# Moving the first score products and the last transposes of u ahead in the full turns of a pipelined language-model tower

## What is computed

```python
h = take(quantised_table, x)
n = layernorm(h)
# mixer on rms(n):
proj = rms(n) @ in_proj_w.T                  # z gate, u, B, C, dt
u, B, C = silu(causal_conv4(u, B, C))        # B and C normalised
z_t = (z + d*(B u - A*y)) / (1 + d*d*A); y_t = y + d*z_t; out = sum(y*C)   # scan over 128 tokens
n = n + (out + D*u) * silu(zgate) @ out_proj_w.T + out_proj_b
n = n + gelu(rms(n) @ fc1_w.T + fc1_b) @ fc2_w.T + fc2_b
h = h + n
out = h + int8_linear(layernorm(h))          # one scale from the largest |value| of all
```

## Time and profile before

| | |
|---|---|
| three executions, us | 1285.45, 1287.50, 1288.92 |
| median | 1287.5 |
| profiled execution | 1287.84 |
| its span, first to last instruction | 1286.0 |
| PE busy | 1149.3 (89%) |
| DVE busy | 1112.5 (87%) |
| ACT busy | 789.0 (61%) |
| POOL busy | 715.1 (56%) |
| mean granted PE clock | 0.990 |

### The profile page before, as it was taken

The page is one execution under the profiler, slowest core; times in us unless marked ns, Lnnn a source line. Parts: engine busy times, 40 slices in busy tenths (PEclk is TensorE's granted clock), DMA queues, the critical chain, the costliest instruction groups (busy, mean ns, idle before and its releaser), DMA issues. The chain is left out here.

```text
span 1286.0 us, 25011 instructions
## 1 busy us (share of the span) xinstructions
PE 1149.3 (89%) x7285; PEld 761.0 (59%) x7292; DVE 1112.5 (87%) x1994; ACT 789.0 (61%) x1275; POOL 715.1 (56%) x2062
## 2 busy tenths in 40 slices
PE   2991075999999999999999999999999999999987
PEld 1550032567676757676666667675767676667554
DVE  5998989979898989898989899998989897887188
ACT  4666747384848484748484757666575747452358
POOL 8882010747585858585858585858575766650000
PEclk9999997899999999999999999999999999999999
DMA  9999901010101010101010100000000101000015
GB/s 354 408 407 418 417 21 36 1 36 1 36 1 36 2 35 0 35 2 34 3 32 8 27 13 22 18 17 18 17 19 16 28 7 34 3 19 1 1 66 196
DMA packets 37169, 91.60 MB, mean 71 GB/s; under 512 B 10173, under 2 KB 21778, under 8 KB 32770
## 3 DMA queue, kind: packets, MB, share of 16 engines
q1 hardware_dynamic: 33474, 81.32, 17.9%
q0 software_dynamic: 3072, 8.39, 1.7%
q10 hardware_dynamic: 576, 1.31, 0.3%
HBM read 81.29 MB, written 9.70 MB: 71 GB/s over the span
## 5 line engine op out<-in xcount | busy, mean ns | idle before, releaser
L804 POOL TENSOR_TENSOR stp<-Gs,X 128x32 f32<-128x32 f32 x900 | 262.7, 292 | 263.1 <-ACT X L777 196.2
L806 POOL TENSOR_TENSOR Gs<-Gs,stp 128x32 f32<-128x32 f32 x900 | 274.4, 305 | 70.4
L1215 PE MATMUL bank<-w_fc,gl 128*128 128x256 f32 x1024 | 242.6, 383 | 0.1
L1196 PE MATMUL bank<-mT,w_fc 128*128 128x512 f32 x512 | 236.7, 595 | 1.8 <-ACT mT L1176 1.7
L1215 PEld LDWEIGHTS bank<-w_fc,gl 128*128 128x128 f32 x1024 | 191.6, 191 | 54.5 <-issue 27.0
L654 PE MATMUL bank<-xT,w_in 128*128 128x512 f32 x448 | 207.3, 603 | 9.0 <-DVE uT L1104 8.9
L966 ACT ACTIVATE uT<-bank,cols 128x512 f32<-128x512 f32 x64 | 47.9, 775 | 224.6 <-DVE sz L1111 134.8
L1196 PEld LDWEIGHTS bank<-mT,w_fc 128*128 128x128 f32 x512 | 94.9, 190 | 85.9 <-issue 79.9
L654 PEld LDWEIGHTS bank<-xT,w_in 128*128 128x128 f32 x448 | 81.8, 191 | 93.1 <-issue 77.8
L980 DVE SCALAR_TENSOR_TENSOR uT<-bank,cols,uT 128x500 f32<-128x500 f32 (+1 forms) x192 | 133.4, 733 | 2.3
L359 DVE TENSOR_TENSOR peak<-ring,peak 128x1536 f32<-128x1536 f32 (+2 forms) x67 | 115.3, 1721 | 9.0 <-ACT ring L258 6.8
(11 more groups left out here) (220 smaller groups left out, 1897.5 us busy)
## 6 DMA issues: line engine op xcount, KB each, us to landing
ring<-in_table SPq DMA_DIRECT2D x31, 1536.0 KB
d_rep<-d_rows SPq DMA_DIRECT2D x128, 64.0 KB, 2.0
out<-res SPq DMA_DIRECT2D x14, 512.0 KB, 2.9
b_rep<-bc_rows SPq DMA_DIRECT2D x128, 32.0 KB, 1.8
c_rep<-bc_rows SPq DMA_DIRECT2D x128, 32.0 KB, 1.8
w_fc<-in_w_fc SPq DMA_DIRECT2D x2, 1024.0 KB, 15.1
ring<-in_table SPq DMA_DIRECT2D x2, 768.0 KB
w_in<-in_w_in ACTq DMA_DIRECT2D x1, 1088.0 KB
```

The source lines that it names most:

```text
L804: pool.tensor_tensor(stp[:], Gs[:, t, ::-1, :], X2[:, t, :, :], ALU.mult).then_inc(rec.sem, 1)
L806: pool.tensor_tensor(Gs[:, t + 1, :, :], Gs[:, t, :, :], stp[:], ALU.add).then_inc(rec.sem, 1)
L1196: last = pe.matmul(pj[n % 4][:, :], w_fc1[:, k, n * P:(n + 1) * P], mT[:, k, :], start=(k == 0), stop=(k == KD - 1))
L1215: last = pe.matmul(sbk[j // 2][:, (j % 2) * D:(j % 2 + 1) * D], gl[n % LEAD][:, j * LEN:(j + 1) * LEN], w_fc2[:, n, :], start=False, stop= ...
```

## The change

In full turns PE issues the transposes of sequences 2 and 3 ahead of fc2 part 5 (before: ahead of part 6), and the first scores ahead of fc2 part 6 (before: ahead of part 7). ACT makes the first two copies to `utok` between gelu parts 6 and 7, and the other two behind part 7 (before: all four there). Turn 1, which has no MLP part, keeps its order. The turn after the last group has a branch of its own, which is not touched.

```diff
-        def act_utok(act, g):
-            act.wait_ge(kq.sem, kq.at(g))
-            if since(g):
-                act.wait_ge(y_mm.sem, y_mm.at(g - 1))
-            for j in range(G):
+        def act_utok(act, g, seqs=range(G)):
+            if 0 in seqs:
+                act.wait_ge(kq.sem, kq.at(g))
+                if since(g):
+                    act.wait_ge(y_mm.sem, y_mm.at(g - 1))
+            for j in seqs:
                 act.wait_ge(u_T.sem, u_T.at(g, j + 1))
...
-                    if second and first and n == FT + 1:
-                        if not third:
-                            pe_warm(pe, sbk[0], 12)
-                        pe_u_T(pe, p, g if first else None, 2)
-                        pe_u_T(pe, p, g if first else None, 3)
-                    if second and first and n == FT + 2:
+                    if second and first and third and n == FT:
+                        pe_u_T(pe, p, g, 2)
+                        pe_u_T(pe, p, g, 3)
+                    if second and first and third and n == FT + 1:
                         pe_scores(pe, p, 0)
-                        if not third:
-                            pe_warm(pe, sbk[0], 4)
+                    if second and first and not third and n == FT + 1:
+                        pe_warm(pe, sbk[0], 12)
+                        pe_u_T(pe, p, g, 2)
+                        pe_u_T(pe, p, g, 3)
+                    if second and first and not third and n == FT + 2:
+                        pe_scores(pe, p, 0)
+                        pe_warm(pe, sbk[0], 4)
                     if third and n >= LEAD:
                         pe_fc2(pe, m, n - LEAD)
...
+                    if second and first and n == FT - 2:
+                        act_utok(act, p, (0, 1))
                 if second and first:
-                    act_utok(act, p)
+                    act_utok(act, p, (2, 3))
```

## The result

The change makes the kernel slower: 1290.08 us in the median of 18 executions against 1286.98 for the kernel before (18), a ratio of 1.0021 with a 95% interval of 1.0014 to 1.0029, so 0.2% slower. Forecast were 1283.6 us and a range of 1281.1 to 1287.2. The profiled execution has a span of 1289.5 (before: 1286.0).

What follows compares the result with a forecast made beforehand. The prediction took TensorE, busy 89% of the span, as the bound, with a 0.62 us wait for VectorE's skip each turn. Saving 14 x 0.28 = 3.9 us from 1287.84 gave 1283.9, by the median 1283.6; range 1281.1 to 1287.2.

Steps and rivals of the forecast that it cites:

- the 0.62 us stall: Each turn PE's projection of u (L654) waits 0.62 us for DVE's skip of tiles 2 and 3.
- Nothing lost between fc2 part 4 and the scan; copies in time: PE's reordered stretch still ends at 616.16, priced at nothing; the copies are done 0.8 us before the scores need them.
- What it is worth, 0.28: First masks start 1.15 us earlier, but second masks wait for unmoved second scores, so 0.28 us a turn reaches PE.
- The 2.18 of the first masks: Lag in us from scores' start to first masks in the loop, used to time the second masks too.
- 2.08: Lag in us from scores' start to masks in turn 2, outside the loop; the forecast used 2.18 instead.
- the printed end: The scores' end shown by the profile, taken as releasing nothing; if it did, the gain would be 0.45 a turn.
- What is late next: At the seam between turns, POOL's rms and ACT's copies leave about 0.26 us; POOL's further loss is counted as 0.
- The sum: Over full turns 2 to 15, 14 x 0.28 = 3.9 us less, giving 1283.6 by the median.
- the second one ("nothing comes of it"): POOL or ACT at the seam becomes the limit, or POOL loses a step; about 1287.5, chance 0.18.
- The third, PE waiting for copies: PE's scores wait for copies 3 and 4; at 1.4 us lateness 4.2 us slower, about 1291.5; chance 0.06.

Runs made afterwards that it cites:

- change_rms46: The changed kernel with POOL's rms factor computed after recurrence step 46 instead of 48; ratio 0.9961 against the kernel before.
- change_rms46_58: The changed kernel with the rms factor after step 46 and 58 instead of 60 recurrence steps on POOL; 1281.71 us, ratio 0.9951 against the kernel before.
- pe_alone: The changed kernel with PE's new order kept but all four copies behind the eighth gelu; ratio 1.0128 against the kernel before.

## Why the prediction was wrong, point by point

- *What bounds the kernel, the 0.62 us stall*: right, and all of the gain that was there. PE's own 61.40 came back as turn less wait for the skip in change_rms46 (61.79 - 0.39) and change_rms46_58 (61.70 - 0.30).
- *Nothing lost between fc2 part 4 and the scan; copies in time*: right. The scan starts at 24.67 after the turn's first transposes in both, and the copies were 0.8 early.
- *What it is worth, 0.28*: right in mechanism, a little small. The second masks start 2.09 after the second scores (619.12 to 621.21), not 2.18, so 0.37 reached PE. The 2.18 of the first masks in the loop was no property of the loop; what it was stays open. 2.08 was the better row, the printed end still not the release.
- *What is late next*: **this step failed.** I put the room at the seam at 0.26 us and POOL's further loss at 0, because "the same DVE operations lie inside POOL's 48 steps before and after". The room was 0.34 (13.01 - 12.67). The loss was 0.59. The operations did stay the same, but how long each stops POOL depends on how much of it is left when POOL's operation begins, and on whether that one is short or the long pow operation, and this I treated as fixed. The bias add came 1.05 us earlier in the turn and was met 0.15 worse; the last two gates came only 0.37 earlier, but from beside the pow operation, where both together cost 0.47, to two short ones, where they cost 0.33 each. A part of 0.1 was there ahead of both and is not explained.
- *The sum*: wanted was the larger of 61.40 + 0.25 and 49.60 + 12.67 = 62.27. I added up the first alone, with 0.34 for the 0.25. Even with POOL's loss at 0 the second is 61.68, so the room allowed just the 0.34 of the gain of 0.37. For 14 turns the second is 0.25 x 14 = 3.5 us above before; measured were 2.95 from turn 1 to turn 16 and 3.1 between the medians.
- *Rivals*: the second one ("nothing comes of it") named the place and the mechanism, POOL losing to DVE's moved operations and PE waiting at L1169 or L1196. It had 0.18, and it stopped at zero gain; nothing in its reason set that floor. The third, PE waiting for copies, did not occur; pe_alone shows its price, 1.3 us a turn.

## What to carry to other kernels

In a pipeline that repeats, find every cycle that could hold the turn and write down the length of each, not only the slack of one wait: here PE's own work with its one wait (62.02 before), POOL's factor to the seam (61.68) and the recurrence through POOL and DVE (up to 61.96 where it showed) lie within 0.4 us of each other, so an edit to one is worth only the distance to the next. When an engine's operations move in time, recount what they do to an engine that shares something with them, operation by operation: an equal number of collisions is not an equal cost. And if a move that should help does not, look for the wait that took its place; an edit of one number (the rms factor two steps earlier) turned this change from 0.2% slower to 0.4% faster.

## What the runs showed of the hardware that was not expected

- A short POOL operation stopped by a DVE operation with two SBUF inputs ends 0.10 to 0.12 us after it, so the cost is what is left of the DVE operation: a bias add of 1.22 us cost one POOL operation 0.88 before and 1.03 after the change (1.13 and 1.28 long, 0.25 alone), two gates of 0.74 each cost 0.33 each, an addition of 0.61 cost 0.20. A multiplication of one SBUF input, 0.41 long, cost nothing. The long pow operation (1.00 alone) lost 0.47 to the first of two gates and nothing to the second, which ran inside it in 0.68.
- These stops hold POOL to DVE's times. POOL's first operation starts at 9.94 to 10.21 after the transposes in nine turns of the kernel before, and the factor at 49.01 or 49.02 in all of them; with the change the factor is at 49.57 to 49.59 in eight turns and one operation later, at 49.92, in one.
- The start of DVE's masks, released by PE's last score matmul, came 2.08 to 2.09 after the block's first matmul in turn 2 and at the second scores in the loop of the changed kernel, and 2.18 at the first scores in the loop of the kernel before, with the block equally long in all.
